# The softmax division of a windowed attention moves from the attention's result to the exponentials, and from VectorE to GpSimd

## The reference, cut to what matters

```python
sim = jnp.einsum('bhwid,bhwjd->bhwij', bq, bk)
sim = jnp.where(mask, -jnp.finfo(sim.dtype).max, sim)
attn = jax.nn.softmax(sim, axis=-1)
out = jnp.einsum('bhwij,bhwjd->bhwid', attn, bv)
```

## Time and profile before

| | |
|---|---|
| median of 3 runs | 1832.1 us (1830.48 to 1832.68) |
| the profiled execution's own time | 1836.2 us |
| its span, first to last instruction | 1834.4 us |
| TensorE matrix work, busy | 1700.3 us (93%) |
| TensorE weight loads, busy | 1016.5 us (55%) |
| VectorE, busy | 1081.9 us (59%) |
| ScalarE, busy | 910.0 us (50%) |
| GpSimd, busy | 173.8 us (9%) |
| mean granted TensorE clock | 0.961 |

### The profile page before, as it was taken

The page is one execution under the profiler, slowest core; times in us unless marked ns, Lnnn a source line. Parts: engine busy times, 40 slices in busy tenths (PEclk is TensorE's granted clock), DMA queues, the critical chain, the costliest instruction groups (busy, mean ns, idle before and its releaser), DMA issues.

```text
span 1834.4 us, 28037 instructions
## 1 busy us (share of the span) xinstructions
PE 1700.3 (93%) x8536; PEld 1016.5 (55%) x8537; DVE 1081.9 (59%) x2991; ACT 910.0 (50%) x2195; POOL 173.8 (9%) x281
## 2 busy tenths in 40 slices
PE   5779997789999999999999999999999999999997
PEld 2558886455555555555555555555555555555565
DVE  7763332476665666556666666566666656565652
ACT  2213332366464747455646464556474646464731
POOL 5023342210020002000200020002000000000000
PEclk8759999799999999999999999999999999999998
DMA  7714443210010011000100110001001000000000
GB/s 232 274 57 130 122 122 78 72 35 12 1 36 1 1 35 35 25 13 1 36 1 1 35 35 24 14 1 36 1 1 35 13 24 1 1 1 1 1 23 12
DMA packets 59107, 72.31 MB, mean 39 GB/s; under 512 B 16644, under 2 KB 44888, under 8 KB 58840
## 3 DMA queue, kind: packets, MB, share of 16 engines
q1 hardware_dynamic: 50088, 58.77, 9.8%
q0 software_dynamic: 5376, 10.76, 2.3%
q10 hardware_dynamic: 3504, 1.06, 0.2%
HBM read 50.64 MB, written 19.92 MB: 38 GB/s over the span
## 4 chain that ended last, share of the span: by engine, by line
PE 72%; DVE 5%; issue 3%; ACT 2%; DMA 0%; POOL 0%; ACTq 0%; DVEq 0%; POOLq 0%
PE pj L1473 18%; PE pj L1561 17%; PE pj L1567 8%; PE pj L1539 6%; PE sp L1497 5%; PE ob L1522 5%; PE sp L1507 4%; PE pj L1481 3%; PE pj L1463 1%; PE pj L1531 1%; DVE ssum L1756 1%; DVE direct L1766 1%; PE pj L1545 1%; PE pj L1549 1%; PE pj L1573 1%
## 5 line engine op out<-in xcount | busy, mean ns | idle before, releaser
L1473 PE MATMUL pj<-wqkv,xT 128*128 128x512 f32 x768 | 348.7, 604 | 6.1 <-issue 5.5
L1561 PE MATMUL pj<-xsq,w 128*128 128x512 f32 (+3 forms) x748 | 325.3, 579 | 7.0 <-DVE hid L1840 4.5
L1642 ACT ACTIVATE prob<-prob,nm 128x256 f32<-128x256 f32 (+1 forms) x512 | 239.2, 469 | 65.5 <-DVE nm L1779 65.3
L1473 PEld LDWEIGHTS pj<-wqkv,xT 128*128 128x128 f32 x768 | 146.6, 195 | 179.8 <-issue 179.8
L1779 DVE CUSTOM_DVE_ANT_0 prob<-sp,mask 128x256 f32<-128x256 f32 (+1 forms) x512 | 167.9, 385 | 112.2 <-issue 112.2
L1561 PEld LDWEIGHTS pj<-xsq,w 128*128 128x128 f32 (+1 forms) x748 | 135.4, 191 | 137.0 <-issue 128.1
L1507 PEld LDWEIGHTS sp<-ident,prob 128*128 128x128 f32 x896 | 107.5, 141 | 91.9 <-issue 70.9
L1522 PE MATMUL ob<-pT,vv 128*64 128x128 f32 x1792 | 120.4, 280 | 28.0 <-DVE pT L1375 21.7
L1567 PE MATMUL pj<-hid,w 128*128 128x512 f32 (+3 forms) x340 | 140.5, 568 | 1.2 <-DVE hid L1840 1.2
L1507 PE MATMUL sp<-ident,prob 128*128 128x128 f32 x896 | 128.2, 275 | 12.9 <-ACT prob L1642 12.9
L1187 PE MATMUL yb<-w2m,hT 128*128 x576 | 135.1, 388 | 1.1 <-DVE yt L1222 0.7
(11 more groups left out here) (307 smaller groups left out, 2290.4 us busy)
## 6 DMA issues: line engine op xcount, KB each, us to landing
w1x<-w_folded SPq DMA_DIRECT2D x72, 128.0 KB, 2.6
slots_y<-yt SPq DMA_DIRECT2D x36, 256.0 KB, 2.2
x1tok<-in_x_dram SPq DMA_DIRECT2D x10, 512.0 KB, 6.8
w1m<-in_L_ffn_w_dram SPq DMA_DIRECT2D x8, 512.0 KB, 6.0
w2m<-in_L_ffn_w_dram SPq DMA_DIRECT2D x8, 512.0 KB, 9.1
x_after_moe<-x1tok SPq DMA_DIRECT2D x8, 512.0 KB
x1out<-x_after_moe SPq DMA_DIRECT2D x8, 512.0 KB, 3.3
out_dram<-x1out SPq DMA_DIRECT2D x7, 512.0 KB, 2.9
```

The costliest lines, as they stand in the source:

```text
L1473: mm = pe.matmul(o[:, :], xs(s, c, w * P, P), wqkv[:, l, c, k * INNER:(k + 1) * INNER], start=(c == 0), stop=(c == DC - 1))
L1561: mm = pe.matmul(o[0:P if j == NJ - 1 else HJ[j], 0:tn], cols, h[:, c, t0:t1], start=(c == 0), stop=(c == DC - 1))
L1642: ins = a.activation(prob[:, g % 4, hh, 0:n], prob[:, g % 4, hh, 0:n], ACT.Exp, bias=nm[:, g % 4, hh:hh + 1], scale=-1.0, accum_out=rs[:, ...
```

## The change

The reciprocals of the sums are taken per four heads, one `rr` step behind each `score` step. GpSimd multiplies the exponentials in `prob` by them, two heads at a time (in window 0 128x256 numbers, else 128x512), and TensorE transposes the quotients: turn_p waits for GpSimd (`divided`) and no longer for the exponentials. The spread copy, `turn_r` and `rb` are gone. `fin` becomes a plain copy of `ob` to `oT`, on ScalarE. The out step puts two windows into one bank for batch slot 1. The order tables are all new; of VectorE's `LATER` table one line is shown before and after.

```diff
 ORDERS = [line.split() for line in """
-    qkv rope score:0 score:1 square_sum rr norm turn_p:0 turn_p:1 turn_p:2 turn_p:3 turn turn_r pv:0 pv:1 fin
-    score:0 score:1 qkv turn_p:0 rope rr turn_p:1 square_sum norm turn_r turn_p:2 turn_p:3 turn pv:0 pv:1
-    score:0 fin' score:1 qkv rr turn_p:0 rope turn_p:1 square_sum turn_p:2 turn_r turn_p:3 norm pv:0 turn pv:1 fin
-    score:0 score:1 turn_p:0 rr qkv turn_p:1 rope square_sum turn_p:2 turn_p:3 turn_r pv:0 norm pv:1 turn fin
+    qkv score:0 rope score:1 rr:0 square_sum rr:1 norm turn_p:0 turn_p:1 turn_p:2 turn_p:3 turn pv:0
+    pv:1' fin' score:0 score:1 qkv rope rr:0 turn_p:0 turn_p:1 rr:1 square_sum norm turn_p:2 turn_p:3 turn pv:0 pv:1 fin
+    score:0 score:1 rr:0 qkv rr:1 turn_p:0 rope turn_p:1 square_sum turn_p:2 norm turn_p:3 pv:0 turn pv:1
+    fin' score:0 score:1 rr:0 qkv rr:1 rope square_sum turn_p:0 turn_p:1 turn_p:2 turn_p:3 pv:0 pv:1 norm fin turn
 """.strip().split("\n")]
...
 def out_steps(s, wins=range(NW)):
-    return [dict(kind="out", s=s, wins=list(wins))]
...
-VECTOR_LATER = {"down": -1, "fin": 6, "fin.0": 7, "fin.1": 5, "fin.2": 1, "fin.3": -3, "gate": 1, "gate.0":
...
+    wins, size = list(wins), 1 + s
+    return [dict(kind="out", s=s, wins=wins, parts=[wins[k:k + size] for k in range(0, len(wins), size)])]
...
+VECTOR_LATER = {"down": -10, "down.0": -3, "down.1": -3, "fin": -16, "fin.0": 2, "fin.1": 13, "fin.2": -4,
...
-        if kind in ("qkv", "rope", "square_sum", "norm", "turn", "turn_r", "rr", "fin"):
+        st["use"] = c.take("use", len(st["parts"]) if kind == "out" else USES.get(kind, 0))
+        if kind in ("qkv", "rope", "square_sum", "norm", "turn", "fin"):
             st["win"] = c.take("win_" + kind, 1)
-        if kind in ("score", "turn_p", "pv"):
-            st["grp"] = c.take("grp_" + kind, 2 if kind in ("score", "pv") else 1)
+        if kind in ("score", "rr", "turn_p", "pv"):
...
-            rr = sb("rr", [P, H])
+            rr = sb("rr", [P, 2, H])
             pT = sb("pT", [P, 4, 2, 2, P])
-            rr_wide = sb("rr_wide", [P, H, DH])
-            rb = sb("rb", [P, IC, P])
...
                         elif kind == "turn_p":
                             g = st["grp"]
-                            pe.wait_ge(exp_done, at(g, i, GRP, 1, 1))
+                            pe.wait_ge(divided, at(g, i, GRP, 1, 1))
                             for hh in range(2):
                                 for k in range(2 if w else 1):
...
-                        elif kind == "turn_r":
-                            pe.wait_ge(inverted, at(st["win"], i, WIN, 2, 2))
-                            o = bank(u, i)
-                            for c in range(IC):
-                                mm = pe.transpose(o[:, c * P:(c + 1) * P],
-                                                  rr_wide[:, 2 * c:2 * c + 2, :].rearrange("p h d -> p (h d)"),
-                                                  ident[:, :])
-                            mm.then_inc(proj_full, 1)
...
-                            for n_, w_ in enumerate(st["wins"]):
+                            for n_, part in enumerate(st["parts"]):
                                 o = bank(u + n_, i)
-                                for c in range(DC):
-                                    mm = pe.transpose(o[:, c * P:(c + 1) * P], xT[s][:, c, 1 + w_ * P:1 + (w_ + 1) * P],
-                                                      ident[:, :])
+                                for k, w_ in enumerate(part):
+                                    for c in range(DC):
+                                        mm = pe.transpose(o[:, k * D + c * P:k * D + (c + 1) * P],
+                                                          xT[s][:, c, 1 + w_ * P:1 + (w_ + 1) * P], ident[:, :])
...
-                        elif kind == "turn_r":
-
-                            wait(a, o_ready, at(st["win"], i, WIN))
-                            o = wait_full(a, u, i)
-                            a.copy(rb[:, :, :], o[:, :].rearrange("p (c t) -> p c t", c=IC)
-                                   ).then_inc(proj_taken[u % NP], 1)
+                        elif kind == "fin":
+                            win = st["win"]
+                            a.wait_ge(pv_done, at(win, i, WIN, 4, 4))
+                            a.copy(oT[:, :, w * P:(w + 1) * P], ob[:, :, :]).then_inc(o_ready, 1)
...
-                        if kind == "pick":
+                        if kind == "rr":
+                            n = 2 * P if st["w"] else P
+                            for par in range(2):
+                                g = st["grp"] + par
+                                pool.wait_ge(inverted, at(g, i, GRP, 1, 1))
+                                by = rr[:, st["win"] % 2, head_of(2 * st["g"] + par, 0):][:, 0:3:2]
+                                pool.tensor_tensor(prob[:, g % 4, :, 0:n], prob[:, g % 4, :, 0:n],
+                                                   by.unsqueeze(2).to_broadcast([P, 2, n]), ALU.mult).then_inc(divided, 1)
+                        elif kind == "pick":
...
                         elif kind == "rr":
-                            win = st["win"]
-                            wait(v, o_ready, at(win, i, WIN))
-                            v.wait_ge(exp_done, at(win, i, WIN, 4, 4))
-                            v.reciprocal(rr[:, :], rs[:, win % 2, :]).then_inc(inverted, 1)
-                            v.wait_ge(inverted, at(win, i, WIN, 2, 1))
-                            v.tensor_copy(rr_wide[:, :, :], rr[:, :].unsqueeze(2).to_broadcast([P, H, DH])
-                                          ).then_inc(inverted, 1)
-                        elif kind == "fin":
-                            win = st["win"]
-                            wait_taken(v, st["turn_r_use"], i)
-                            v.wait_ge(pv_done, at(win, i, WIN, 4, 4))
-                            v.tensor_tensor(oT[:, :, w * P:(w + 1) * P], ob[:, :, :], rb[:, :, :], ALU.mult
-                                            ).then_inc(o_ready, 1)
+                            g, win = st["grp"], st["win"]
+                            v.wait_ge(exp_done, at(g, i, GRP, 1, 2))
+                            heads = slice(4 * st["g"], 4 * st["g"] + 4)
+                            v.reciprocal(rr[:, win % 2, heads], rs[:, win % 2, heads]).then_inc(inverted, 2)
                         elif kind == "wo":
```

More of the change, by code:

```diff
@@ L206, in head_of @@
     return 4 * (g // 2) + g % 2 + 2 * hh
-USES = dict(qkv=3, turn=2, turn_r=1, wo=1, mean=1, var=1, gate=1, value=1, down=1, load=DC, rotate=DC, lead=1, lead_rot=1, out=NW)
+USES = dict(qkv=3, turn=2, wo=1, mean=1, var=1, gate=1, value=1, down=1, load=DC, rotate=DC, lead=1, lead_rot=1)
 def number(steps, c):
@@ L218, in number @@
         kind, s = st["kind"], st["s"]
-        st["use"] = c.take("use", len(st["wins"]) if kind == "out" else USES.get(kind, 0))
-        if kind in ("qkv", "rope", "square_sum", "norm", "turn", "turn_r", "rr", "fin"):
+        st["use"] = c.take("use", len(st["parts"]) if kind == "out" else USES.get(kind, 0))
+        if kind in ("qkv", "rope", "square_sum", "norm", "turn", "fin"):
             st["win"] = c.take("win_" + kind, 1)
-        if kind in ("score", "turn_p", "pv"):
-            st["grp"] = c.take("grp_" + kind, 2 if kind in ("score", "pv") else 1)
+        if kind in ("score", "rr", "turn_p", "pv"):
+            st["grp"] = c.take("grp_" + kind, 1 if kind == "turn_p" else 2)
             st["win"] = st["grp"] // 4
@@ L235, in number @@
         st["outs"] = c.take("outs", kind == "out" and st["wins"][-1] == NW - 1)
-        for what in ("qkv", "turn", "turn_r", "wo", "gate", "value", "load", "lead"):
+        for what in ("qkv", "turn", "wo", "gate", "value", "load", "lead"):
             st[what + "_use"] = c.n.get("last_" + what)
         st["x_use"] = c.n.get(f"last_x{s}")
-        if kind in USES:
+        if kind in USES or kind == "out":
             c.n["last_" + kind] = c.n["use"] - 1
@@ L268, in schedule @@
     per = {k: c.n[k] - start.get(k, 0) for k in c.n if not k.startswith("last_")}
-    for what in ("qkv", "turn", "turn_r"):
+    for what in ("qkv", "turn"):
         assert c.n["last_" + what] - start["last_" + what] == per["use"], what
@@ L1321, in build @@
             inverted = sem("inverted")
+            divided = sem("divided")
             o_ready = sem("o_ready")
@@ L1404, in one @@
                             w0, w1_ = st["wins"][0], st["wins"][-1] + 1
-                            wait_taken(sp, st["use"] + len(st["wins"]) - 1, i)
+                            wait_taken(sp, st["use"] + len(st["parts"]) - 1, i)
                             sp.dma_start(out[i * 2 + st["outs"]].rearrange("(w p) d -> p w d", p=P)[:, w0:w1_, :],
@@ L1851, in one @@
                             v.wait_ge(reloaded, at(st["outs"], i, OUTS, 16, 16))
-                            for n_, w_ in enumerate(st["wins"]):
+                            for n_, part in enumerate(st["parts"]):
```

(3 more changed lines are left out.)

17 lines of the change are left out of this document (10 added, 7 removed), and 37 rows, old and new, of tables (SCALAR_LATER, VECTOR_LATER).

## The result

The changed kernel takes 1871.07 us (median of 4 runs, 1868.65 to 1874.66) against 1832.39 (4 runs, 1830.48 to 1833.49). The ratio is 1.0214, with a 95% interval from 1.0195 to 1.0233: 39 us slower. Its profiled execution took 1874.66 us with a span of 1872.9, 38.5 longer than the span of before.

What follows compares the result with a forecast made beforehand. TensorE was taken as the limit, with ScalarE-VectorE chains binding at windows 0 and 3. Terms -13.2 + 21.0 + 4.5 + 13.7 + 8.1 + 5 - 2 = +37.1 gave 1869 us; range 1808 to 1900.

Steps and rivals of the forecast that it cites:

- Price of a multiply: GpSimd's added products: 1.27 us estimated for 128x512, from a slope between two measured lengths; 0.73 for 128x256.
- Holding: VectorE operations reading SBUF twice wait up to one multiply when they meet a GpSimd product.
- Rival 1: Nothing on VectorE is held by GpSimd's products, wide operations running side by side: 1827 us; chance 0.19.
- Window 0: In 15 stages, a later norm and multiplies beside rope's add, sum and norm: 15 x 1.4 = +21.0 us.
- The order's 0.3: In window 0, norm behind the second wo add and its sum delays the next scores: +0.3 us, turn_r's gain included.
- Windows 1 and 2: TensorE stays busy and saves turn_r's transposes, 30 x 0.44 = -13.2 us; hnorm meeting a multiply in window 1, +4.5.
- the -2 of the forecast: Out's slot 1 takes two banks in place of four, saving waits of 0.44 us for VectorE's add: -2 us.
- Window 3: At its end rope meets the multiplies: 1.8 us of holding, +1.3 at 8 ends, +0.55 at 6, together +13.7 us.
- Picks: GpSimd issues them behind window 3's last multiply, so VectorE's mix and rope wait: six picks, +8.1 us.
- First stage: The second pick stands ahead of window 2's reciprocals with no feed-forward to cover it: 4 to 8, +5 us taken.
- Rival 2: TensorE stays the limit everywhere, no chain decides, and turn_r's whole 28.2 us come off: 1802 us; chance 0.15.
- Rival 3: The pick decides: six picks cost their upper 4.2 us each and the first 8: 1889 us; chance 0.10.

Runs made afterwards that it cites:

- experiments 2 and 3: 2: the changed kernel, GpSimd multiplying one column of each head, 1837.1 us; 3: the kernel before plus GpSimd products nobody waits for, picks issued ahead, 1862.9 us.
- experiment 4: The changed kernel with pv.3.0 done twice on TensorE in each of 16 windows 3: 1861.9 us, ratio 1.0146.
- experiment 5: The changed kernel with picks issued ahead, pv.3.0 done twice, and the first stage's pick mix ahead of window 2's masks: 1839.3 us, ratio 1.0036.
- experiment 1: The changed kernel with GpSimd's picks issued ahead of window 2's first division of the stage before: 1853.1 us, ratio 1.0111.

## Why the prediction was right in the sum, and where its steps were wrong

The direction and the total came as forecast (1869, measured 1871). That the total came so near is luck: its terms were wrong by up to 11 us, on both sides. The mechanism named first, GpSimd's products holding up VectorE in the chains at the windows' ends, is real, as experiments 2 and 3 show, but it was priced too high; and the largest loss, TensorE's lower clock behind its new waits, was no term at all. An estimate of it from the tables: some 15 us in windows 3 (21.4 less the 6.2 of experiment 4) and 8 to 9 in windows 0 behind a pick (four of them grew by 2.1 more than the two without a fall), 24 of the 39 us.

- **Price of a multiply**: 1.27 us forecast, 1.22 measured in the mean, 1.01 to 1.25 by what ran beside it. Right.
- **Holding**, read off a single row of a small operation: right for wide ones. Rope, hnorm and the sum behind wo were all longer, and back to their old lengths with one column; rope's add and norm hardly changed (1238 and 1240 ns for 1214 and 1225). Rival 1 falls.
- **Window 0**, 15 x 1.4 = 21.0 forecast: 9.7 measured apart from the picks. The order's 0.3 was too small: with one column it still costs 0.4 to 0.5. Holding was far too dear: 1.1 forecast, about 0.2 measured (0.65 less 0.45).
- **Windows 1 and 2**, -13.2 + 4.5 forecast: -18.1 measured. The 0.44 of turn_r came off in window 1 to the hundredth. Window 2 gained more, 0.6 to 0.7, and 1.15 in the stages [0,0], where out's two windows to a bank fall (the -2 of the forecast). hnorm was held as feared (749 to 1140 ns), but under cover, and cost nothing.
- **Window 3**, +13.7 forecast: 21.4 measured. The chain alone, as experiment 4 shows it with most of the clock's loss gone, costs 6.2. Where no fall of the clock disturbs them, the nine are at +0.5 to +0.6 (experiment 5) and with one column at -0.5, the gain forecast for no holding; so the products' length costs 1.1 there, where 1.8 of holding was taken. The step that failed is the one that priced TensorE's waits by their length alone: the lower clock behind them cost up to 2.5 us a window, and the prediction had no term for it.
- **Picks**, 8.1 forecast: 18 measured by the medians, 14.3 in windows 0 (experiment 1). The mechanism was right, the size was off. The fetch took 15.9 us where 13.3 had been read from the earlier trace rows, since GpSimd's two small products and two of its issues were themselves held, 2.6 us together. And four of the six windows had a lower clock as well (0.67 granted from 532.4 to 536.6 in the one of +3.81); the two without grew by only 1.0 more than windows 0 without a pick.
- **First stage**, 5 forecast: 9.4 measured, and not by the pick: moving its parts left window 2's 5.3 as it was. TensorE waits there for quotients whose exponentials stand late on ScalarE (experiment 5).
- **Rival 2**, TensorE remaining the limit everywhere, holds in windows 1 and 2 only. **Rival 3** was half right: the pick was the largest single loss that one edit undoes.

The Trainium skill's page SBUF — State Buffer, section "Who interferes with whom", says that a VectorE instruction with two SBUF inputs contends with a GpSimd instruction that reads SBUF. Rope's swapped part agrees: 2.12 us for 1.28 beside products of 1.25.

## What to carry to other kernels

Work given to an idle GpSimd is not free for VectorE: count each VectorE operation with two SBUF inputs that may fall beside it, and put the work into stretches where TensorE has other things to do, as windows 1 and 2 had here. In a stream that is taken in order, look at what else queues behind the new work: moving the picks ahead of it gave back 18 of the 39 us here. Where a change lets the limiting engine wait more often, read its granted clock behind the waits, and split the change by stage: half of it may be worth keeping, as it was here.

## What was not expected of the hardware

The granted clock of TensorE fell from 1.00 to 0.50 about three waits of 0.83, 1.09 and 1.84 us with work between them, in nine windows of nine; with the last two alone in four of nine; and before, with 0.4 and 1.45 us, in one of nine. Repeating 1.09 us of work that was already done, in one of these waits, made the kernel 9 us faster. And holding goes both ways: an indirect DMA's issue on GpSimd took 1.90 and 1.70 us beside rope's add and norm on VectorE, where 0.95 is usual. The kernel before shows it as well (1.97 beside rope, 1.70 beside norm).
